# First group normalization: four batches of images in place of three, and five images' statistics on ScalarE

## The reference

```python
# x: (32 images, 32, 32, 128 channels) float32; C = 128, G = 32 groups of 4 channels
def gn(v):        # over all 1024 positions and the 4 channels of a group, for each image
    g = v.reshape(B, H, W, 32, 4)
    return ((g - mean(g, (1, 2, 4))) / sqrt(var(g, (1, 2, 4)) + 1e-5)).reshape(v.shape)

def layer0(x, acc):     # acc: (32, 32, 128, 128), a 128x128 matrix for each of 1024 positions
    log_w = log_softmax(log(acc), axis=2)
    # log of a product of exponentials, for each position over the channels
    return log(einsum('vhbk,vhks->vhbs', exp(x - x_max), exp(log_w - w_max))) + x_max + w_max

def layer1(x, ...):     # attention with 1024 tokens an image, then LayerNorm and leaky ReLU
    nf = x / max(norm(x), 1e-12)
    A  = softmax(5 * (nf @ adj_w @ nf.T))
    h  = A @ (x @ affine_w.T + affine_b)
    return leaky_relu(layernorm(h) * ln_g + ln_b)

x = x + layer0(gn(x), acc)
x = x + layer1(gn(x), ...)
```

## Time and profile before

| | us |
|---|---|
| median of 3 runs | 1132.06 |
| the three runs | 1131.41, 1132.06, 1136.18 |
| profiled execution, its own time | 1137.41 |
| its span, from the first to the last instruction | 1135.7 |
| TensorE busy | 1048.5 |
| ScalarE busy | 915.5 |
| VectorE busy | 828.5 |
| GpSimd busy | 553.6 |
| first product of the second stage starts at | 59.36 |

### The profile page before, as it was taken

How to read it: one execution, slowest core, us unless ns; L and a number is a source line. 1 busy time by engine, 2 the same in 40 slices (tenths; PEclk the granted TensorE clock), 3 DMA queues, 4 the chain that set the end, 5 groups by cost and what they waited for, 6 DMA issues and landing times.

```text
span 1135.7 us, 20986 instructions
## 1 busy us (share of the span) xinstructions
PE 1048.5 (92%) x7392; PEld 792.3 (70%) x7392; DVE 828.5 (73%) x1577; ACT 915.5 (81%) x1806; POOL 553.6 (49%) x391
## 2 busy tenths in 40 slices
PE   0199999948999999999999999999999999999995
PEld 0155555536777777777777777777778777777773
DVE  7813545568877777787787778787777777777776
ACT  0499999537888888888888888888888888888885
POOL 0045444403355555555555555555555555555533
PEclk9999999969999999999999999999999999999998
DMA  8979999830122222223322222222222222222212
GB/s 356 388 302 407 400 382 409 330 130 19 63 78 75 76 77 82 75 76 116 146 81 87 76 76 75 75 88 82 81 88 76 84 77 75 75 82 79 75 57 95
DMA packets 46903, 158.15 MB, mean 139 GB/s; under 512 B 5848, under 2 KB 6732, under 8 KB 36556
## 3 DMA queue, kind: packets, MB, share of 16 engines
q1 hardware_dynamic: 46796, 156.78, 36.9%
HBM read 136.45 MB, written 20.31 MB: 138 GB/s over the span
## 4 chain that ended last, share of the span: by engine, by line
PE 85%; DVE 7%; DMA 5%; ACT 2%; issue 1%; POOL 0%; SPq 0%; POOLq 0%; DVEq 0%; ACTq 0%
PE PS L1137 23%; PE PS L1138 21%; PE PS L1139 21%; DMA Wt<-acc 5%; PE PS L1155 5%; PE PS L1114 4%; DVE st L685 4%; PE PS L1104 3%; PE PS L1149 3%; PE PS L1125 2%; PE PS L1143 2%; PE PS L1172 0%; DVE Pl L852 0%; ACT Ph L529 0%; ACT ET L454 0%
## 5 line engine op out<-in xcount | busy, mean ns | idle before, releaser
L852 DVE TENSOR_TENSOR Pl<-PS,Ph 128x512 fp32r<-128x512 f32 x512 | 347.6, 689 | 111.2 <-ACT PS L530 106.6
L530 ACT ACTIVATE PS<-PS 128x512 f32<-128x512 f32 x512 | 302.3, 600 | 0.7 <-PE PS L1139 0.5
L529 ACT ACTIVATE Ph<-PS 128x512 fp32r<-128x512 f32 x384 | 229.1, 596 | 58.5 <-PE PS L1139 58.1
L1137 PE MATMUL PS<-Ph,hh 128*128 128x512 f32 x512 | 210.3, 411 | 0.2 <-DVE Pl L852 0.2
L1137 PE MATMUL PS<-uTh,nTh 128*128 128x512 f32 x512 | 200.5, 392 | 0.9 <-DVE uTl L831 0.9
L1138 PE MATMUL PS<-Pl,hh 128*128 128x512 f32 x512 | 200.5, 392 | 0.0
L1139 PE MATMUL PS<-Ph,hl 128*128 128x512 f32 x512 | 200.1, 391 | 0.0
L1138 PE MATMUL PS<-uTl,nTh 128*128 128x512 f32 x512 | 199.9, 390 | 0.0
L1139 PE MATMUL PS<-uTh,nTl 128*128 128x512 f32 x512 | 199.9, 390 | 0.0
L412 POOL TENSOR_TENSOR X<-X 128x512 f32<-128x512 f32 x62 | 79.4, 1281 | 247.1 <-DVE X L874 247.1
L378 POOL TENSOR_TENSOR LL<-LL 128x512 f32<-128x512 f32 x64 | 82.5, 1288 | 143.3 <-ACT LL L462 143.3
(11 more groups left out here) (126 smaller groups left out, 1708.4 us busy)
## 6 DMA issues: line engine op xcount, KB each, us to landing
Wt<-acc SPq DMA_DIRECT2D x64, 1024.0 KB, 7.6
X<-x SPq DMA_DIRECT2D x16, 1024.0 KB, 19.6
out<-X SPq DMA_DIRECT2D x64, 256.0 KB, 2.0
X<-factor_rows SPq DMA_DIRECT2D x63, 256.0 KB, 3.1
NU<-factor_rows SPq DMA_DIRECT2D x63, 256.0 KB, 3.5
SQ<-norm_rows SPq DMA_DIRECT2D x31, 512.0 KB, 3.5
out<-X SPq DMA_DIRECT2D x6, 512.0 KB, 4.7
X<-out SPq DMA_DIRECT2D x6, 512.0 KB, 6.5
```

What stands on the lines that cost most here:

```text
L529: act.activation(Ph[:, g % RING, :], sl, ACT.Exp, scale=SHARP)
L530: act.activation(sl, sl, ACT.Exp, scale=SHARP).then_inc(weights_ready, 1)
L852: dve.tensor_tensor(Pl[:, r, :], SL[r], Ph[:, r, :].bitcast(F32), ALU.subtract)\
L1137: pe.matmul(out_, lh, rh, start=start, stop=False)
```

## The change

The first turn gets four batches, of 10, 10, 8 and 4 images. VectorE no longer takes the pieces of images 2, 5, 12, 15 and 21. ScalarE takes their sums with an Identity over the 1024 positions that also gives the sum of its results (`accum_out`), makes the negative mean, takes the sum of squares around it with Square, and writes both in the slots of `st` where the batch's steps look for them. Each image is five instructions, and each but the second small copy waits for the one before it by the new semaphore `act_steps`. The images of a batch stand in ScalarE's program ahead of the roots of their batch, so behind the exponentials of the batch before. VectorE waits for them in `batch_sums`.

The order on VectorE changes too: sums and squares of a batch stand together behind the pieces of its last load (4, 9 and 13), variances and scales behind the pieces of the next load. The last batch stands behind all pieces, as before. The second turn's batches get the numbers 4 and 5 in place of 3 and 4, with nothing else changed.

```diff
-BATCHES = ((0, 0, 16), (0, 16, 26), (0, 26, 32), (1, 0, 4), (1, 4, 32))
+BATCHES = ((0, 0, 10), (0, 10, 20), (0, 20, 28), (0, 28, 32), (1, 0, 4), (1, 4, 32))
+EARLY, REST = 4, 5
+
+BY_ACT = ((2, 5), (12, 15), (21,), ())
...
+        asum = sb("asum", [P, 3 * sum(map(len, BY_ACT))])
...
+            def statistics(j, b):
+
+                total, mean_, square = [asum[:, 3 * j + i:3 * j + i + 1] for i in range(3)]
+                slots = st[:, b, 0:PIECES[0], :].rearrange("p m (e s) -> p m e s", s=3)
+                dump = ET[:, 1, 0:8, :].rearrange("p b n -> p (b n)")
+
+                def spread(col):
+                    return col.unsqueeze(2).broadcast_to([P, PIECES[0], 2])
+
+                act.wait_ge(image_loaded[b // IPL], 16)
+                if j:
+                    act.wait_ge(act_steps, 5 * j)
+                act.activation(dump, X[:, b, :], ACT.Identity, accum_out=total).then_inc(act_steps, 1)
+                act.wait_ge(act_steps, 5 * j + 1)
+                act.activation(mean_, total, ACT.Copy, scale=-1.0 / NPOS).then_inc(act_steps, 1)
+                act.activation(slots[:, :, :, 1], spread(total), ACT.Copy, scale=1.0 / NPOS).then_inc(act_steps, 1)
+                act.wait_ge(act_steps, 5 * j + 3)
+                act.activation(dump, X[:, b, :], ACT.Square, bias=mean_, accum_out=square).then_inc(act_steps, 1)
+                act.wait_ge(act_steps, 5 * j + 4)
+                act.activation(slots[:, :, :, 2], spread(square), ACT.Copy, scale=1.0 / (2 * PIECES[0]))\
+                    .then_inc(act_steps, 1)
...
-            for i in range(3):
+            for i in range(EARLY):
+                for j, b in enumerate(BY_ACT[i]):
+                    statistics(sum(map(len, BY_ACT[:i])) + j, b)
                 roots(i)
                 act.wait_ge(stat_steps, NS * (i + 1))
                 exps(0, range(*BATCHES[i][1:]))
...
             def batch_sums(i):
                 _, lo, hi = BATCHES[i]
                 dve.wait_ge(stat_pieces, i + 1)
+                if i < EARLY:
+
+                    dve.wait_ge(act_steps, 5 * sum(map(len, BY_ACT[:i + 1])))
...
                 for b in range(i * IPL, (i + 1) * IPL):
-                    for m in range(PIECES[0]):
-                        done = piece(0, m, b)
-                if (i + 1) * IPL in [hi for _, _, hi in BATCHES[0:3]]:
+                    if b not in sum(BY_ACT, ()):
+                        for m in range(PIECES[0]):
+                            done = piece(0, m, b)
+                if (i + 1) * IPL in [hi for _, _, hi in BATCHES[:EARLY]]:
                     done.then_inc(stat_pieces, 1)
 
-                for at, batch in ((7, 0), (12, 1)):
+                for batch in range(EARLY - 1):
+                    at = BATCHES[batch][2] // IPL - 1
                     if i == at:
                         batch_sums(batch)
+                        batch_squares(batch)
                     if i == at + 1:
-                        batch_squares(batch)
-                    if i == at + 2:
                         batch_variances(batch)
                         batch_scales(batch)
-            batch_sums(2)
-            batch_squares(2)
-            batch_variances(2)
-            batch_scales(2)
+            batch_sums(EARLY - 1)
+            batch_squares(EARLY - 1)
+            batch_variances(EARLY - 1)
+            batch_scales(EARLY - 1)
...
-            for i in range(3):
+            for i in range(EARLY):
                 for h in (0, 1):
                     sum_groups(i, h)
```

More of the change, by code:

```diff
@@ L160, in build @@
         stat_pieces = sem("stat_pieces")
+        act_steps = sem("act_steps")
         away_read = sem("away_read")
@@ L223, in sums_of @@
         def sums_of(i):
-            return W1 if i == 4 else W0
+            return W1 if i == REST else W0
         def norms_of(b):
@@ L299, in load_rq @@
                 else:
-                    sp.wait_ge(stat_steps, 5 * NS)
+                    sp.wait_ge(stat_steps, (REST + 1) * NS)
                 sp.dma_start(fac_of(n), factor_rows[n, 1:2, :].broadcast_to([P, HW])).then_inc(rq_loaded[e], 16)
@@ L436, in _ @@
             with pool.Else():
-                pool.wait_ge(stat_steps, 5 * NS)
+                pool.wait_ge(stat_steps, (REST + 1) * NS)
         @block.scalar
@@ L480, in token_squares @@
                 if b == 0:
-                    act.wait_ge(stat_steps, 4 * NS)
+                    act.wait_ge(stat_steps, (EARLY + 1) * NS)
                 elif b == 1:
@@ L485, in token_squares @@
                 else:
-                    if b == BATCHES[3][2]:
-                        act.wait_ge(stat_steps, 5 * NS)
+                    if b == BATCHES[EARLY][2]:
+                        act.wait_ge(stat_steps, (REST + 1) * NS)
                     act.wait_ge(nT_ready, b - 1)
@@ L566, in opening @@
             def opening():
-                roots(3)
+                roots(EARLY)
                 token_squares(0)
@@ L606, in attention @@
                             if k == 14:
-                                roots(4)
+                                roots(REST)
                         if k == 0 and b >= 2:
@@ L801, in first_statistics @@
                 last_pieces(0, 4).then_inc(stat_pieces, 1)
-                batch_sums(3)
+                batch_sums(EARLY)
                 last_pieces(B - AWAY, B - AWAY + 2)
-                batch_squares(3)
+                batch_squares(EARLY)
                 last_pieces(B - AWAY + 2, B).then_inc(away_read, 1)
-                batch_variances(3)
-                batch_scales(3)
+                batch_variances(EARLY)
+                batch_scales(EARLY)
             def tokens(b):
@@ L951, in attention @@
                             if k == 10:
-                                batch_sums(4)
+                                batch_sums(REST)
                             if k == 11:
-                                batch_squares(4, away=True)
+                                batch_squares(REST, away=True)
                             if k == 13:
-                                batch_variances(4)
+                                batch_variances(REST)
                             if k == 15:
-                                batch_scales(4)
+                                batch_scales(REST)
                         if k == (0 if b else 2) and b + 1 < B:
@@ L1067, in _ @@
                 last_pieces(4, B - AWAY).then_inc(stat_pieces, 1)
[L1068 to L1072, removed]
+                batch_sums(REST)
+                batch_squares(REST)
+                batch_variances(REST)
+                batch_scales(REST)
+                dve.wait_ge(stat_steps, (REST + 1) * NS)
                 general()
@@ L1200, in values @@
                     if b == 2:
-                        pe.wait_ge(stat_steps, 4 * NS + 8)
+                        pe.wait_ge(stat_steps, REST * NS + 8)
                 values_into(W1, ZT[b % 2], e).then_inc(values_made, 1)
@@ L1243, in opening @@
                 for h in (0, 1):
-                    sum_groups(3, h)
+                    sum_groups(EARLY, h)
                 norms(0)
@@ L1276, in attention @@
                                 pe.wait_ge(hf_ready, 4)
-                                sum_groups(4, 0)
+                                sum_groups(REST, 0)
                             if k == 15:
-                                sum_groups(4, 1)
+                                sum_groups(REST, 1)
                         if k == (0 if b else 2) and b + 1 < B:
@@ L1347, in _ @@
             with pe.Else():
-                for i in (3, 4):
+                for i in (EARLY, REST):
                     for h in (0, 1):
```

## The result

The changed kernel takes 1136.19 us in the median of 22 runs, the one before 1133.34 in 22 runs beside them. The ratio is 1.0028, with a 95% interval from 1.0019 to 1.0036: slower by 3.2 us (2.2 to 4.1), under half a per cent. The prediction said 2.8 us later. Its time, 1134.9, started from a median of three runs (1132.06); with 19 runs more that median is 1133.34, and this accounts for the 1.3 us between 1134.9 and 1136.19.

A forecast was written before the change was run, and what follows sets the result against it. The opening up to the first product was taken to bound the change: -3.6 pieces, +4.8 batches, +2.8 wait, -0.8 exponentials, -0.4 other = +2.8 us, on 1132.06 giving 1134.9 us; range 1130.3 to 1139.3.

The forecast's parts named there:

- First sums at 20.6, images 2 and 5 worth nothing: In the opening's load-paced stretch, moving these images off VectorE only gives it idle time; first sums start at 20.6 us.
- 3.6 us saved by three images, 4.8 us lost by the batches: On VectorE, images 12, 15 and 21 save 3.6 us of pieces; the batches' steps cost 4.8 us more.
- ScalarE's image at 3.03 us: Five steps on ScalarE take 3.03 us an image, with bounds of 2.8 and 3.5.
- VectorE waits 2.8 us for image 15: At batch 1's sums VectorE waits 2.8 us, as ScalarE takes images 12 and 15 behind ten exponentials.
- Image 21 is in time by 0.2: ScalarE ends image 21 at 47.91 us, VectorE its 12 pieces at 48.14, so no wait there.
- First product at 62.17: TensorE's first product, L1114, starts at 62.17 us against 59.36 before, 2.8 us later.
- One to one to the end: Later stages have no slack, so a microsecond at the first product is a microsecond at the end.
- a change in the second stage's length: Sign of being wrong: the stage behind the first product was to stay as long as before.
- The table switch: Mechanism on ScalarE: a table load there and back makes an image 5.6 us, +10.3 us, 1142.4 us in all.
- the second rival: ScalarE's images are dearer, so VectorE waits longer at sums of batches 1 and 2: middle case 1139 us, chance 0.10.
- ScalarE was late: Its rival: an image costs ScalarE 1.6 us or less, no wait, first product at 59.4, 1132.1 us; chance 0.12.
- The floor of the third: Rival that VectorE gains: last landing sets the first product at 54.3 us, 5.0 earlier, 1127.0 us; chance 0.06.

The follow-up runs named there:

- The test with one more image: The changed kernel with image 16 also on ScalarE, behind images 12 and 15: ratio 1.0051 against the kernel before, first product at 65.09 us.
- the kernel with the earlier image: The changed kernel with image 10 replacing 12, ahead of batch 0's roots, and VectorE waiting for images only in their own batch: ratio 0.9994 against the kernel before.
- The nine rows beside the one of before: Table of the change and eight follow-up kernels against the kernel before, each with its first product and measured ratio, from 0.9959 to 1.0051.
- with images 16 and 26: The kernel before, with its three batches and order, but only images 16 and 26 on ScalarE: 1129.62 us, ratio 0.9959; repeated, 0.9964.

## Why the prediction was right

- **First sums at 20.6, images 2 and 5 worth nothing.** 20.59, and the same with these images on VectorE. Right, and tested.
- **3.6 us saved by three images, 4.8 us lost by the batches.** The direct counterpart is the kernel without images on ScalarE, which the forecast doesn't name. Its terms for the batches, the exponentials and the longer batch of before, 4.8 - 0.8 - 0.4, give 3.6 us later, and 3.6 was measured. Spacing its steps gave back 2.5 us at the last sums (57.22 to 54.72): 0.79 and 0.77 for the first two batches, near the 0.75 of one cover, and 0.92 for the third, whose last pieces no longer stand right ahead of the last sums. Right.
- **ScalarE's image at 3.03 us.** 3.07. The Square with one column as operand took 1.149 and Identity 1.050, where I had taken 1.14 and 1.05.
- **VectorE waits 2.8 us for image 15.** 2.93, at 36.48 where 36.39 was forecast. The test with one more image moved it by 2.9, and that with an earlier image took it away.
- **Image 21 is in time by 0.2.** It ended at 47.80 + 0.21 = 48.01, the sums started at 48.29. Right, with 0.28.
- **First product at 62.17.** 62.22. That it fits to 0.05 is in part luck, for two small errors cancel: the last sums came 0.13 later than forecast (56.47 against 56.34), and from them to the exponentials it took 4.05 (56.47 to 60.52) where 4.14 was taken from a batch of six. The mechanism doesn't hang on either.
- **One to one to the end.** The ratio, 3.2 us (2.2 to 4.1), holds the 2.9 of the first product. The nine rows beside the one of before bear it out. A single profile doesn't: a change in the second stage's length was named as a sign of being wrong, and it fell from 173.8 to 172.2 us. The last section says why this is put down to the execution.
- **The table switch.** There is one load of 1.283 us in the changed kernel too, so that mechanism of the second rival didn't occur. The rule of the Trainium skill (ScalarE: Activation LUTs, "Table sets: the hidden batching unit") had nothing to act on here, since all five functions run under the set that is held.
- **The rivals.** ScalarE was late, its images weren't dearer, and VectorE gained nothing. Images 2 and 5 were done on ScalarE at 16.76, long before 20.6; the forecast says 16.7, though its own landing of 10.4 and 3.03 us an image give 16.5, and nothing rests on it. The floor of the third, 54.3 us for a last batch of four, was approached only by other choices: 56.69 with a last batch of six.

## What to carry to other kernels

Work moved to an idle engine has to be idle time at the right place: look at what stands ahead of it in that engine's program and who waits behind it. Here five images, 15 us of ScalarE's time, gave back only 0.8 of the 3.6 us that the batches lost: two of them were taken where VectorE needed no relief, and two stood behind ten exponentials. Two other images, 6 us in ScalarE's gaps, brought the first product forward by 2.7 us and the end by 4.1 to 4.7. Count an engine's load only from where it lags behind the transfers; what was taken from it before that point was worth nothing. And each batch more costs its fixed chain (3.3 us here, 0.75 less with other work between its steps), so a smaller last batch pays only if it saves more than that; here it saved two exponentials, 0.8 us. Four batches with their steps spaced and with images taken in time were not run, so whether a fourth batch can pay here stays open.

## What the runs showed of the hardware that was not expected

The second stage's length differs from profile to profile by more than this change is worth, with the same work in it. From the first product to the second turn's first sums on TensorE it took 173.8 us before (59.36 to 233.19), 172.2 after (62.22 to 234.38) and 169.3 in the kernel with the earlier image (59.16 to 228.48); over all eleven profiles it lies between 168.4 and 174.4. If the 4.5 us between the first and the third belonged to the kernel, its median would be as much lower; it is 0.7 us lower (0.9994), and at the end of its interval 2.9. So most of it belongs to the execution. The one program that was profiled twice, with images 16 and 26, took 168.4 and 169.1. The windows from 68 to 190 us, of before, and of the kernel with the earlier image (length, busy time of each engine, clock, DMA share, GB/s):

```profile
68.00:190.00 122.00, 118.18 (x2060) 68.36 (x2060) 52.95 (x110) 116.78 (x235) 60.31 (x47) 1.00 0.99 398
```

```profile
68.00:190.00 122.00, 120.52 (x2115) 70.37 (x2116) 54.97 (x114) 119.84 (x242) 62.09 (x48) 1.00 1.01 411
```

The DMA engines are busy all the time in both (0.99 and 1.01) and moved 398 against 411 GB/s. From 60 to 224 us, TensorE's weight loads and matmuls waited less for weights from memory (total, times, longest; the two can overlap):

```profile
PEld PS L1104 <- DMA Wt<-acc: 8.1, 14, 1.3
PE PS L1104 <- DMA Wt<-acc: 4.7, 8, 1.1
```

```profile
PEld PS L1137 <- DMA Wt<-acc: 3.7, 7, 0.7
PE PS L1137 <- DMA Wt<-acc: 1.9, 6, 0.5
```

Both first products start within 0.2 us of each other, so their starting time doesn't explain it. What does stays open: slower transfers can be the cause, or the effect of later requests, since a chunk is asked for only when its slot is free. It is why the two profiles of before and after differ by only 1.5 us in span, while the 22 runs of each put the change at 3.2: the first product is 2.9 later, the second stage 1.7 shorter, and what follows 0.3 longer.
